# Routed experts: every token to its two experts in 39 sorted tiles, instead of all eight experts over all tokens

## The chip, the cores and the metric

One Trainium2 chip; the kernel runs on one of its cores. The metric is the device time of one execution in microseconds (us), as the median of several runs.

## What is computed

A tensor of 8 images of 16x16 tokens, 192 channels wide (2,048 tokens in all), passes through four layers: windowed attention with an MLP (layer 0), attention behind a group norm (layer 1), causal attention (layer 2) with a mixture of experts, and a last attention with a parallel block. All values are float32. The change is in the mixture of experts, which the reference computes for every token and every expert, and of which it keeps two:

```python
def _L2_ffn_ref(hidden_states, router_w, w1, w2):      # w1 (8, 512, 192), w2 (8, 192, 512)
    probs = jax.nn.softmax(flat @ router_w.T, axis=-1)
    topk_probs, topk_idx = jax.lax.top_k(probs, TOP_K)  # TOP_K = 2
    importance = probs.sum(axis=0)
    ...
    balanced = topk_probs / running[topk_idx]
    balanced = balanced / balanced.sum(axis=-1, keepdims=True)
    h = jax.nn.silu(jnp.einsum('th,eih->tei', flat, w1))
    outs = jnp.einsum('tei,ehi->teh', h, w2)
    sel = jnp.take_along_axis(outs, topk_idx[:, :, None], axis=1)
    return (sel * balanced[..., None]).sum(axis=1)
...
t = t + _L2_attn_ref(_ln_t(t), ...)
t = t + _L2_ffn_ref(_ln_t(t), ...)
t = t + _L3_attn_ref(_ln_t(t), ...)
```

## The kernel before

The kernel holds all tokens in `xall` (128 partitions x 16 rows of 192) and works on them in turns of two images, 512 tokens or 4 rows of `xall` (TURNS = 4, TT = 4). It has three parts, each a fixed order of instructions per engine, tied by semaphores.

Part A runs layers 0 to 2 up to the router. `round_a` interleaves the attention of one image (`paired`: scores, row maxima on VectorE, exponentials on ScalarE, values) with the side chains `chain_a1` to `chain_a3` of the other (projections, norms, layer 0's MLP). `chain_a3` ends with the router's probabilities in `pall`. VectorE's row maxima (`neg`) release the next scores on TensorE. GpSimd computes only 1/sqrt of the variances (`rstd_b`, `rstd_groups`) and copies for the padded windows.

The expert part is dense. After all four turns VectorE sums `pall`, TensorE sums it over partitions, and VectorE makes the weights `rrun`. Then VectorE normalises the four rows of a turn into `xd`, TensorE transposes them (`over`, L952 and L955), and for each of the 8 experts TensorE runs `up` (8 matmuls of 512 columns, four of them on half the contraction rows, weights in `moe1` and `moe1b`) and `down` (16 matmuls of 192 columns, weights in `moe2`), with `up` of the next expert ahead of `down`. A float32 matmul is two passes in the trace, so `up` is 16 and `down` 32 of them. ScalarE applies silu to four 128x512 banks per expert (L1271), VectorE multiplies with the token's weight for that expert and adds (L1908, four instructions per expert); `gates` computes these weights, zero for experts that were not chosen. All expert weights lie in SBUF: SyncE loads them once, `moe1`, `moe1b` and the first five experts of `moe2` during the last turn of part A, the other three when its last projection is done (L435 to L439). The weights of part B (`loads_b`) are loaded at the kernel's start.

Part B runs the last attention and its parallel block in the same manner as part A. `first_b` normalises the next turn's rows; its statistics on VectorE (`moments`) stand in VectorE's order ahead of row maxima. Each turn's result is stored from SyncE.

## Time and profile before

| | us |
|---|---|
| median of 3 runs | 2143.72 (2131.91 to 2151.96) |
| the profiled execution, whole | 2142.87 |
| its span in the trace | 2140.9 |
| TensorE matmul busy | 1959.9 (92%) |
| VectorE, ScalarE, GpSimd busy | 769.4, 595.4, 76.2 |
| DMA moved | 24.77 MB |

Times in the trace count from the span's start. Busy times of TensorE are of pipelined matmuls whose ends are modelled; how fast passes follow one another is read from their starts. The granted clock is the share of TensorE's full 2.4 GHz: 0.50 is 1.2 GHz. A number in brackets behind a row is the idle time of the engine before it and what ended it.

### The profile page before, as it was taken

The numbers are of one execution on the slowest core, as the hardware profiler recorded it, in microseconds if no ns is written. First come the engines' busy times: TensorE is split into PE (matmuls) and PEld (weight loads), VectorE is DVE, ScalarE is ACT, GpSimd is POOL, SyncE is SP. The second block draws the span as 40 slices with busy tenths as digits, with TensorE's granted clock in tenths as the row PEclk, the third lists the DMA queues.
The fourth block names the chain that finished last, engine by engine and source line by source line (L and its number), as shares of the span: only waits on it lengthen the run. The fifth ranks groups of instructions, "written<-read, shape, count | busy, mean of one in ns | idle before, by whom it ended". The sixth has DMA issues, their size and how long they took to land.

```text
span 2140.9 us, 35201 instructions
## 1 busy us (share of the span) xinstructions
PE 1959.9 (92%) x15802; PEld 1449.4 (68%) x15802; DVE 769.4 (36%) x1975; ACT 595.4 (28%) x919; POOL 76.2 (4%) x112
## 2 busy tenths in 40 slices
PE   6989998899989999898997899999979999999988
PEld 5767777677677776677775566666646666767666
DVE  3233334323433323432343221222125546445462
ACT  1132231332323223223222212112123434333332
POOL 0000000000000000000000000000000001000010
PEclk8799999999999999989998899999978999999999
DMA  8000000000000000000002000000010000000000
GB/s 236 1 1 1 1 1 1 1 1 1 1 1 1 1 1 1 2 1 2 1 34 86 0 1 1 1 1 0 5 35 1 1 8 1 1 8 1 9 1 8
DMA packets 8297, 24.77 MB, mean 12 GB/s; under 512 B 1001, under 2 KB 6092, under 8 KB 7155
## 3 DMA queue, kind: packets, MB, share of 16 engines
q1 hardware_dynamic: 8148, 22.54, 3.4%
q8 instruction: 124, 2.03, 0.4%
q14 instruction: 25, 0.20, 0.0%
HBM read 20.96 MB, written 1.57 MB: 11 GB/s over the span
## 4 chain that ended last, share of the span: by engine, by line
PE 83%; DVE 12%; ACT 3%; issue 1%; DMA 0%; POOL 0%; SPq 0%; DVEq 0%; ACTq 0%; POOLq 0%
PE ps L453 71%; DVE neg L1503 5%; PE ps L683 3%; PE ps L673 3%; PE ps L570 2%; ACT ring L1043 1%; PE ps L628 1%; PE ps L484 1%; PE ps L525 1%; DVE neg L1501 1%; PE ps L860 1%; PE ps L513 1%; DVE moms L1566 1%; DVE neg L1500 1%; ACT ou L1058 1%
## 5 line engine op out<-in xcount | busy, mean ns | idle before, releaser
L1043 ACT ACTIVATE ring<-ps 128x1024 f32<-128x1024 f32 (+1 forms) x240 | 232.7, 980 | 436.6 <-PE ps L453 363.6
L1503 DVE TENSOR_REDUCE neg<-ps 128x4 f32<-128x1024 f32 x192 | 234.5, 1225 | 273.3 <-PE ps L453 273.1
L453 PE MATMUL ps<-kz,qt 32*128 32x256 f32 x1152 | 167.7, 419 | 45.0 <-DVE negp L1495 22.6
L453 PE MATMUL ps<-qt,rw 128*128 128x512 f32 (+1 forms) x512 | 192.2, 632 | 0.9 <-DVE qt L1857 0.9
L453 PEld LDWEIGHTS ps<-lw,zone 128*128 128x128 f32 x1024 | 165.6, 190 | 21.2 <-issue 21.2
L453 PE MATMUL ps<-xt,lw 97*128 97x256 f32 x672 | 172.6, 409 | 7.8 <-ACT xp L1122 4.7
L453 PE MATMUL ps<-lw,zone 128*128 128x192 f32 x1024 | 174.4, 329 | 0.0
L453 PE MATMUL ps<-qm,kz 32*128 32x256 f32 x1152 | 167.6, 421 | 4.5 <-ACT pkp L1043 2.4
L453 PEld LDWEIGHTS ps<-xt,lw 97*128 97x128 f32 x672 | 130.2, 201 | 41.1 <-ACT xt L1078 9.7
L453 PEld LDWEIGHTS ps<-kz,qt 32*128 32x128 f32 x1152 | 93.9, 194 | 83.3 <-DVE neg L1503 30.2
L1908 DVE SCALAR_TENSOR_TENSOR x<-ps,cw,x 128x192 f32<-128x192 f32 x128 | 44.5, 411 | 280.1 <-PE ps L453 280.1
L453 PE MATMUL ps<-ident 128*128 128x256 f32 x472 | 144.1, 399 | 0.0
L1271 ACT ACTIVATE zone<-ps 128x512 f32<-128x512 f32 x128 | 69.5, 594 | 267.1 <-PE ps L453 267.1
L453 PEld LDWEIGHTS ps<-qt,rw 128*128 128x128 f32 (+1 forms) x512 | 64.8, 189 | 109.7 <-issue 109.7
L453 PE MATMUL ps<-rw,relt 32*128 32x256 f32 (+1 forms) x864 | 127.3, 401 | 0.7 <-ACT xt L1078 0.7
L453 PEld LDWEIGHTS ps<-qm,kz 32*128 32x128 f32 x1152 | 93.2, 195 | 23.4 <-issue 12.1
L453 PE MATMUL ps<-ring,v 128*32 128x256 f32 (+1 forms) x1536 | 103.4, 375 | 1.2 <-ACT ring L1043 1.2
L453 PE MATMUL ps<-relt,rw 32*128 32x256 f32 x768 | 103.4, 398 | 0.0
L1078 ACT ACTIVATE xt<-ps 97x512 f32<-97x512 f32 x72 | 42.9, 596 | 216.6 <-PE ps L628 216.6
L453 PEld LDWEIGHTS ps<-rw,relt 32*128 32x128 f32 (+1 forms) x864 | 86.5, 202 | 10.2 <-issue 4.0
L1305 POOL TENSOR_TENSOR rstds<-ves,nhalf 128x2 f32<-128x2 f32 x56 | 39.1, 698 | 1393.8 <-DVE ves L1573 1393.8
L453 PEld LDWEIGHTS ps<-ident 128*128 128x128 f32 x472 | 76.5, 192 | 16.4 <-issue 12.7
(228 smaller groups left out, 2809.5 us busy)
## 6 DMA issues: line engine op xcount, KB each, us to landing
lw<-in_lw SPq DMA_DIRECT2D x3, 720.0 KB
rw<-in_relw SPq DMA_DIRECT2D x1, 2048.0 KB
rw<-in_moe SPq DMA_DIRECT2D x1, 2048.0 KB, 7.6
lw<-in_moe SPq DMA_DIRECT2D x1, 1920.0 KB, 13.9
rw<-in_relw SPq DMA_DIRECT2D x1, 1792.0 KB
out<-xall SPq DMA_DIRECT2D x4, 384.0 KB, 2.6
lw<-in_lwb SPq DMA_DIRECT2D x1, 1440.0 KB
fc<-in_fc SPq DMA_DIRECT2D x2, 576.0 KB
```

Source lines behind the costliest of these rows:

```text
L453: return pe.matmul(o, w, m, start=start, stop=stop)
L484: last = pe.matmul(ps[:, b + j, half * 128:half * 256 + 128], qb[r, im, s, hs], kb[r, im, s, 0:128 + 128 * half], start=False, stop=True, ...
L513: last = pe.matmul(ps[:, b + j, half * NTOK:NTOK + half * 128], kb[r, im, s, hs], qm[r, s, half * 128:NTOK], start=False, stop=True, skip_ ...
L570: last = pe.transpose(ps[:, 5, half * 128:half * 128 + 128], neg[:, s % 2, half, :], ident[:, :])
L673: last = pe.matmul(o[:, :, k, :], rwt[:, 0, at % l.rel, :], qi[:, :, at, :], start=k == 0, stop=True, skip_group_check=True)
L683: last = pe.matmul(o[:, :, :, k], rwt[:, 1, at % l.rel, :], qi[:, :, :, at], start=k == 0, stop=True, skip_group_check=True)
L1043: act.activation(dst, src, ACT.Exp).then_inc(*q.adds("exp_done"))
L1078: act.activation(xt[:, :, im * NTOK:(im + 1) * NTOK], ps[0:CH + 1, 6:8, 0:NTOK], ACT.Copy)\
L1271: act.activation(hid2[:, 4 * (e % 2) + m, :], ps[:, m, :], ACT.Silu).then_inc(*q.adds("h_ready"))
L1305: pool.tensor_tensor(rstds2[:, part, i2], ves[:, part, i2], nhalf[:, 0:2], ALU.pow)\
L1503: ins = dve.tensor_reduce(at, ps[:, b:b + 2, :].rearrange("p j (f k) -> p j f k", f=2), AX.X, ALU.max, negate=True)
L1908: ins = dve.scalar_tensor_tensor(out=dst, in0=ps[:, 4 + 2 * (e % 2) + i // 2, (i % 2) * D:(i % 2 + 1) * D], scalar=cw[:, i, e:e + 1], in1= ...
```

## The change

The dense part goes, and a routed one takes its place. VectorE picks the two experts of each token (`choose`), TensorE counts with a triangular matrix of ones how many tokens ahead of it chose the same expert (`ranks`), and VectorE makes from it the row (`slot`) at which a token's normalised row goes in a new buffer in HBM, `rows_by_expert`: each expert has 16 tiles of 128 rows. GpSimd writes the rows there by indirect DMAs of 128 rows (`scatter`), 32 in all; the 24 of the first three turns are issued during the last turn of part A, 8 behind it. The buffer is filled with zeros first, at the kernel's start (nine stores of SyncE out of a tile that GpSimd clears). From the counts VectorE makes a `table`: for each of 39 tiles (32 full ones and up to 7 begun) its first row in the buffer and the offsets of its expert's weights. 39 tiles always run.

For each tile SyncE reads two numbers of the table into registers and fetches the tile's rows (96 KB) and its expert's first matrix (384 KB) into one of four buffers each; TensorE transposes the rows (`turn`), runs `up` (8 matmuls of 128 columns) and `down` (4 matmuls of 192 columns, whose weights it picks in `moe2` by a register); ScalarE applies silu once (128x512) and issues the store of the tile's result, back to the tile's own rows in HBM, two tiles behind (`keep`); VectorE copies out of PSUM twice per tile. When all 39 stores have landed, GpSimd gathers each token's two results by indirect DMAs, 8 per turn (`gather`), and `first_b` adds them to the token, weighted, in four instructions of VectorE per image. `loads_b` now stands between the fourth and the fifth fetch in SyncE's order.

```diff
+TILES = 2 * B * NTOK // 128 + E2 - 1
+PLACES = B * NTOK // 128
+ALL = TURNS * TT
+LATE = ALL - TT
...
+            sp.wait_ge(blank, 1)
+            for e in range(E2):
+                rows = placed_rows[e * PLACES * 128:(e + 1) * PLACES * 128, :]
+                sp.dma_start(rows.rearrange("(p n) d -> p (n d)", p=128), late[:, 0:PLACES * D]).then_inc(zeroed, 16)
...
+            sp.wait_ge(tabled, 1)
+            sp.wait_ge(scattered, 16 * 2 * ALL)
+            def fetch(k):
+                if k >= 4:
+                    sp.wait_ge(turned, k - 3)
+                place = sp.value_load(table[0:1, 0, k:k + 1], min_val=0, max_val=(PLACES * E2 + E2 - 2) * 128)
+                sp.dma_start(xin[:, k % 4, :], placed_rows[bass.ds(place, 128), :]).then_inc(tile_in[k % 4], 16)
+                if k >= 4:
+                    sp.wait_ge(up_mm, k - 3)
+                row = sp.value_load(table[0:1, 2, k:k + 1], min_val=0, max_val=CH * (E2 - 1))
+                sp.dma_start(moe1[:, k % 4, :, :], a["moe1"][bass.ds(row, CH), :, :]).then_inc(w_in[k % 4], 16)
+            for k in range(4):
+                fetch(k)
...
             for dst, src in loads_b:
                 sp.dma_start(dst, src).then_inc(ld_b, 16)
...
+            for k in range(4, TILES):
+                fetch(k)
+            sp.wait_ge(down_mm, TILES)
...
+            ranks(LATE, ALL, 2)
+            pe.wait_ge(counted, 1)
+            mm(ps[:, 6, 400:400 + E2], ones[:, :], count[:, 1, :]).then_inc(count_mm, 1)
...
+            def turn(k):
+                if k >= 2:
+                    pe.wait_ge(xts_ready, k - 1)
+                pe.wait_ge(tile_in[k % 4], 16 * (k // 4 + 1))
+                for c in range(2):
+                    last = pe.transpose(ps[0:CH, k % 2, c * 128:(c + 1) * 128], xin[:, k % 4, c * CH:(c + 1) * CH],
+                                        ident[:, :])
+                last.then_inc(turned, 1)
+            def up(k):
+                pe.wait_ge(w_in[k % 4], 16 * (k // 4 + 1))
+                if k >= 2:
+                    pe.wait_ge(hds_ready, k - 1)
+                pe.wait_ge(xts_ready, k + 1)
+                for m in range(4):
+                    for c in range(2):
+                        last = mm(ps[:, 2 + k % 2, m * 128:(m + 1) * 128],
+                                  moe1[:, k % 4, c, m * 128:(m + 1) * 128], xts[:, k % 3, c, :],
+                                  c == 0, c == 1)
+                last.then_inc(up_mm, 1)
+            def down(k):
+                first = pe.value_load(table[0:1, 1, k:k + 1], min_val=0, max_val=4 * D * (E2 - 1))
+                if k >= 2:
+                    pe.wait_ge(y_ready, k - 1)
+                pe.wait_ge(hds_ready, k + 1)
+                for m in range(4):
+                    last = mm(ps[:, 4 + k % 2, 0:D], hds[:, k % 3, m, :],
+                              moe2[:, bass.ds(first + m * D, D)], m == 0, m == 3)
+                last.then_inc(down_mm, 1)
+            pe.wait_ge(ld_moe, 32)
+            pe.wait_ge(tabled, 1)
+            turn(0)
+            turn(1)
+            up(0)
+            for k in range(TILES):
+                if k + 2 < TILES:
+                    turn(k + 2)
+                if k + 1 < TILES:
+                    up(k + 1)
+                down(k)
...
+            act.wait_ge(tabled, 1)
+            def keep(k):
+                place = act.value_load(table[0:1, 0, k:k + 1], min_val=0, max_val=(PLACES * E2 + E2 - 2) * 128)
+                act.wait_ge(y_ready, k + 1)
+                act.dma_start(placed_rows[bass.ds(place, 128), :], yst[:, k % 4, :]).then_inc(tile_out[k % 4], 16)
+            for k in range(TILES):
+                act.wait_ge(up_mm, k + 1)
+                if k >= 3:
+                    act.wait_ge(down_mm, k - 2)
+                act.activation(hds[:, k % 3, :, :].rearrange("p m t -> p (m t)"), ps[:, 2 + k % 2, :], ACT.Silu)\
+                    .then_inc(hds_ready, 1)
+                if k >= 2:
+                    keep(k - 2)
+            keep(TILES - 2)
+            keep(TILES - 1)
...
+            def scatter(t0, t1, n):
+                pool.wait_ge(placed, n)
+                for t in range(t0, t1):
+                    for k in range(2):
+                        pool.indirect_dma_start(placed_rows[:, :], bass.IndirectOffsetOnAxis(slot[:, k, t:t + 1], 0),
+                                                xl[:, t, 0:D], None).then_inc(scattered, 16)
+            def gather(turn):
+                if turn >= 2:
+                    pool.wait_ge(combined, IMGS * (turn - 1))
+                for im in range(IMGS):
+                    for i in (2 * im, 2 * im + 1):
+                        for k in range(2):
+                            pool.indirect_dma_start(
+                                gy[:, turn % 2, k, i, :], None, placed_rows[:, :],
+                                bass.IndirectOffsetOnAxis(slot[:, k, turn * TT + i:turn * TT + i + 1], 0))\
+                                    .then_inc(gathered[turn % 2][im], 16)
...
+                    if not more:
+                        scatter(im * LATE // 2, (im + 1) * LATE // 2, 1)
...
+            scatter(LATE, ALL, 2)
+            for n, landed in enumerate(tile_out):
+                pool.wait_ge(landed, 16 * len(range(n, TILES, 4)))
+            gather(0)
...
+            gather(1)
             for t in range(TURNS - 1):
                 q.stage(t, t + 1)
                 for im in range(IMGS):
                     rstd_b(q, 1, im)
                     chain_b1(q, im)
+                if t + 2 < TURNS:
+                    gather(t + 2)
...
+                if q.turn == TURNS - 1 and im == 0:
+                    choose(0, LATE)
...
+                dve.wait_ge(gathered[q.coming % 2][im], 16 * 4 * (q.coming // 2 + 1))
+                for k in range(2):
+                    for i in (2 * im, 2 * im + 1):
+                        t = q.coming * TT + i
+                        ins = dve.scalar_tensor_tensor(out=xall[:, t, :], in0=gy[:, q.coming % 2, k, i, :],
+                                                       scalar=share[:, k, t:t + 1], in1=xall[:, t, :], op0=ALU.mult,
+                                                       op1=ALU.add)
+                    ins.then_inc(*((q.adds("dve_step"), (combined, 1))[k]))
+                    dve.wait_ge(*((q.own("dve_step") if k == 0 else (combined, IMGS * q.coming + im + 1))))
...
+            after(dve.tensor_reduce(count[:, 0, :], both[:, 0:LATE, :].rearrange("p t e -> p e t"), AX.X, ALU.add))
+            choose(LATE, ALL)
+            dve.wait_ge(chosen, 2)
+            dve.tensor_reduce(count[:, 1, :], both[:, :, :].rearrange("p t e -> p e t"), AX.X, ALU.add)\
+                .then_inc(counted, 1)
...
+            read_ranks(LATE, ALL, 2)
+            place(LATE, ALL)
...
+            def turned_in(k):
+                dve.wait_ge(turned, k + 1)
+                if k >= 3:
+                    dve.wait_ge(up_mm, k - 2)
+                dve.tensor_copy(xts[:, k % 3, :, :].rearrange("p c t -> p (c t)"), ps[0:CH, k % 2, 0:256])\
+                    .then_inc(xts_ready, 1)
...
+            for k in range(TILES):
+                if k + 2 < TILES:
+                    turned_in(k + 2)
+                dve.wait_ge(down_mm, k + 1)
+                if k >= 4:
+                    dve.wait_ge(tile_out[k % 4], 16 * (k // 4))
+                dve.tensor_copy(yst[:, k % 4, :], ps[:, 4 + k % 2, 0:D]).then_inc(y_ready, 1)
```

TensorE, the expert part of before from its first transposes: `ps` is PSUM, `qt` holds the transposed tokens, `rw` and `lw` the weights, `zone` the hidden rows.

```order
L952 MATMUL ps<-ident,kz 128x128 [waits m_rows_ready,imp_done,ld_moe]
L952 MATMUL ps<-ident,kz 128x128 x3
L955 MATMUL ps<-ident,kz 128x128 x4
L453 MATMUL ps<-qt,rw 128x512 [waits m_xt1_ready,m_xt0_ready]
L453 MATMUL ps<-qt,rw 128x512 x7
L453 MATMUL ps<-qt,rw 128x512 [waits m_h_ready]
L453 MATMUL ps<-qt,rw 128x512 x3
L453 MATMUL ps<-qt,rw 128x512 [waits m_h_ready]
L453 MATMUL ps<-qt,rw 128x512 x3
L453 MATMUL ps<-lw,zone 128x192 [waits m_acc_done]
L453 MATMUL ps<-lw,zone 128x192 x15
```

TensorE now, one tile in the middle of the 39: `ring` holds the fetched and the transposed rows, the hidden rows and the results, `rw` the first matrix, `lw` all second matrices.

```order
L1029 MATMUL ps<-ident,ring 96x128 [waits tile_in1,xts_ready]
L1029 MATMUL ps<-ident,ring 96x128
L506 MATMUL ps<-ring,rw 128x128 [waits xts_ready,hds_ready,w_in0]
L506 MATMUL ps<-ring,rw 128x128 x7
L1046 TENSOR_LOAD table
L1046 ISA x2
L506 ISA [waits hds_ready,y_ready]
L506 MATMUL ps<-lw,ring 128x192
L506 ISA
L506 MATMUL ps<-lw,ring 128x192
L506 ISA
L506 MATMUL ps<-lw,ring 128x192
L506 ISA
L506 MATMUL ps<-lw,ring 128x192
```

An expert of a turn had 24 matmuls and no register work; a tile has two transposes, 12 matmuls, one load of a register and six register operations, four of them between the matmuls of `down`.

SyncE now, where the tile loop begins: the fourth fetch, `loads_b`, the fifth fetch.

```order
L480 TENSOR_LOAD table
L480 ISA x2
L481 ISA
L481 DMA ring<-rows_by_expert 128x192
L484 TENSOR_LOAD table
L484 ISA x2
L485 ISA
L485 DMA rw<-in_moe1 96x1024
L490 DMA late<-in_lwb 96x3840
L490 DMA late<-in_lwb 1x3840
L490 DMA gb3<-in_gb3 128x384
L490 DMA ties<-in_ties 128x512
L480 TENSOR_LOAD table [waits turned]
L480 ISA x2
L481 ISA
L481 DMA ring<-rows_by_expert 128x192
L484 TENSOR_LOAD table [waits up_mm]
L484 ISA x2
L485 ISA
L485 DMA rw<-in_moe1 96x1024
```

Of these rows only `loads_b` was there before, at the kernel's start; each fetch is two register loads, six register operations and two DMAs, and the transfers of `loads_b` stand ahead of the fifth fetch.

GpSimd now, from the last 1/sqrt of part A to the first turn of part B (`late` is the normalised tokens, `rw` here the buffer of gathered results).

```order
L1375 TENSOR_TENSOR rstds2<-ves,nhalf 128x2 [waits a_var_ready] x4
L1356 DMA rows_by_expert<-late,slot 17280x192 [waits placed]
L1356 DMA rows_by_expert<-late,slot 17280x192 x7
L1366 DMA rw<-rows_by_expert,slot 128x192 [waits tile_out2,tile_out3,tile_out1,tile_out0]
L1366 DMA rw<-rows_by_expert,slot 128x192 x7
L1375 TENSOR_TENSOR rstds2<-ves,nhalf 128x2 [waits b_n_var,set_b]
L1375 TENSOR_TENSOR rstds2<-ves,nhalf 128x2 [waits b_n_var]
L1366 DMA rw<-rows_by_expert,slot 128x192 x8
```

Before, one 1/sqrt per turn of the expert part (`rstd`) stood here; now 8 scatters and 8 gathers stand ahead of part B's first 1/sqrt.

## Rows read from the trace of the kernel before

**Rows 1.** Stretches: from:to, length, busy PE PEld DVE ACT POOL, clock, DMA share, GB/s
```profile
1176.00:1190.00 14.00, 6.89 (x16) 3.74 (x18) 9.18 (x42) 1.88 (x2) 1.01 (x1) 0.50 0.00 0
1200.00:1211.00 11.00, 11.00 (x50) 7.16 (x48) 1.39 (x4) 2.17 (x4) 0.00 (x0) 1.00 0.01 1
1185.60:1548.00 362.40, 362.36 (x1560) 232.29 (x1560) 74.76 (x261) 71.48 (x132) 3.02 (x3) 0.99 0.00 1
```

**Rows 2.** Timeline from the router's end to the first expert: start, us, what
```profile
1175.65 0.17 DVE L1689 TENSOR_TENSOR pall<-ge,gs 128x16 f32<-128x16 f32 x1
...
1182.80 1.09 PE L952 MATMUL ps<-ident,kz 128*128 128x128 f32 x4 [5.85 <-DVE kz L1396]
...
1183.68 1.06 PE L955 MATMUL ps<-ident,kz 128*128 128x128 f32 x4
...
1185.61 14.73 PE L453 MATMUL ps<-qt,rw 128*128 128x512 f32 x32 [0.88 <-DVE qt L1857]
```

**Rows 3.** Timeline of one expert: down, the next expert's up, the next down
```profile
1200.28 5.47 PE L453 MATMUL ps<-lw,zone 128*128 128x192 f32 x32
...
1205.58 5.91 PE L453 MATMUL ps<-qt,rw 128*128 128x512 f32 x16
...
1211.42 3.84 PE L453 MATMUL ps<-lw,zone 128*128 128x192 f32 x22
```

**Rows 4.** Timeline from the last expert to part B's first matmul
```profile
1548.08 1.39 DVE L1908 SCALAR_TENSOR_TENSOR x<-ps,cw,x 128x192 f32<-128x192 f32 x4 [3.81 <-PE ps L453]
...
1551.43 0.62 DVE L1566 BATCH_NORM_STATS2 moms<-xall 128x6 f32<-128x192 f32 x2 [0.27 <-DVE gl L1939]
...
1554.23 1.14 PE L806 MATMUL ps<-ident,xn 128*97 128x128 f32 x4 [6.26 <-DVE xn L1587]
```

**Rows 5.** Groups by shape, expert part: line, shapes, count, busy, mean ns, idle
```profile
L453 PE MATMUL ps<-lw,zone 128*128 128x192 f32 x1024 | 174.4, 329 | 0.0
```

**Rows 6.** Timeline: eight weight loads for the router's matmuls of 8 columns
```profile
1172.67 1.78 PEld L453 LDWEIGHTS ps<-rout,xt 96*128 96x128 f32 x8 [1.03 <-ACT xt L1078]
```

**Rows 7.** SyncE's stores with a register address: ns min/median/max, and landing
```profile
L445 SPq FUSED_REGOPS  x4: 74/74/84, 1747.0 to 2137.7; - x4
...
L445 SPq DMA_DIRECT2D out<-xall x4: 379/402/429, 1747.2 to 2137.8; - x4
...
DMA to landing us min/median/max: 2.6/2.6/2.7
```

**Rows 8.** Waits of SyncE: line, waited for, us in total, times, longest
```profile
SPq L274 <- DMA out<-xall: 2.1, 1, 2.1
```

**Rows 9.** Timeline: SyncE issues three loads of the expert weights, first and last
```profile
1118.15 0.33 SPq L435 DMA_DIRECT2D rw<-in_moe  x1
...
1118.99 1.31 SPq L437 DMA_DIRECT2D lw<-in_moe  x1
```

**Rows 10.** DMA issues: out<-in, engine, count, KB each, median us from issue to landing
```profile
lw<-in_moe SPq DMA_DIRECT2D x1, 1920.0 KB, 13.9
...
xall<-in_x SPq DMA_DIRECT2D x1, 384.0 KB, 3.4
```

**Rows 11.** Timeline: GpSimd in part A's last turn, two instructions in succession
```profile
995.68 1.01 POOL L1322 TENSOR_TENSOR rstd<-ve,nhalf 128x4 f32<-128x4 f32 x1 [28.52 <-DVE ve L1646]
1034.99 0.69 POOL L1305 TENSOR_TENSOR rstds<-ves,nhalf 128x2 f32<-128x2 f32 x1 [38.30 <-DVE ves L1573]
```

**Rows 12.** Timeline: the first and the last of twelve small VectorE instructions that pick experts
```profile
1186.40 0.19 DVE L1867 TENSOR_REDUCE gm<-cw 128x4 f32<-128x32 f32 x1
...
1188.86 0.19 DVE L1883 TENSOR_TENSOR oh<-oh 128x32 f32<-128x32 f32 x1
```

**Rows 13.** Timeline: part B, row maxima behind first_b of image 0 and image 1
```profile
1748.20 1.22 DVE L1503 TENSOR_REDUCE neg<-ps 128x4 f32<-128x1024 f32 x1
...
1749.47 1.13 PE L453 MATMUL ps<-lw 32*128 32x256 f32 x8 [1.03 <-DVE neg L1503]
...
1788.44 1.23 DVE L1503 TENSOR_REDUCE neg<-ps 128x4 f32<-128x1024 f32 x1 [2.27 <-PE ps L453]
```

More of the change, by code:

```diff
@@ L1646, in chain_a1 @@
                 dve.tensor_scalar(ve[0:CH, 0:2], gvar, 1e-5, None, ALU.add).then_inc(*q.adds("gvar_ready"))
+                routed = q.turn == TURNS - 1 and im == 0
+                if routed:
+                    read_ranks(0, LATE, 1)
                 yield
@@ new lines, in _ @@
+            place(LATE, ALL)
+            here, until, tile = (steps0[0:1, u:v] for u, v in ((0, PLACES), (PLACES, PLACES + E2 * E2),
+                                                              (PLACES + E2 * E2, PLACES + E2 * E2 + TILES)))
+            full = steps[:, 0:E2 * PLACES].rearrange("p (e j) -> p e j", e=E2)
+            used, ends, first, own, start, at = (spans[:, 64 * n:64 * n + z] for n, z in enumerate(
+                (E2, E2, E2 * E2, TILES, TILES, TILES)))
+            sums = first.rearrange("p (e f) -> p e f", e=E2)
```

331 lines of the change are left out of this document (147 added, 184 removed).

## Prediction

> **What bounds the kernel now.** I read the stretches first, for the size of the part that is replaced, then the timeline at its two ends and through one expert, for how its time is made up. From the first `up` at 1185.6 to the last `down` at 1548 TensorE is busy 362.36 of 362.40 us at a granted clock of 0.99, while VectorE and ScalarE stand at 75 and 71 us and nothing is transferred [rows 1]. Nobody is waited for: the 1024 passes of `down` have 0.0 us of idle time before them [rows 5]. From one `down` to the next go 11.14 us, 5.30 for its 32 passes and 5.84 for the 16 passes of the next `up` [rows 3]; 32 experts and turns make 356. So this part costs what its passes cost, and fewer passes are fewer microseconds, until something else has to be waited for. At its ends TensorE stands almost still: from `pall` at 1175.65 to the first `up` at 1185.61 [rows 2], and from the last additions at 1548.08 to part B's first matmul at 1554.23 [rows 4].
>
> **What a tile costs TensorE.** A pass of 192 columns takes 5.30/32 = 0.165 us [rows 3], so 0.86 ns a column and 0.11 for 128 columns. Could loading the weights be slower than that? The eight loads of the router's matmuls take 1.78 us, 0.22 each, with next to nothing to multiply [rows 6]; four transposes just behind, at a granted clock of 0.50 [rows 1], also take 0.22 each, from 1182.80 to 1183.68 [rows 2]. Load and 128 columns weigh the same, so 0.11 holds at full clock. A tile has 2 transposes (one pass each, 0.22), 8 matmuls of 128 columns (16 passes, 1.76) and 4 of 192 (8 passes, 1.32): 3.30 us. Between the matmuls of `down` stand four register operations of about 0.07 [rows 7], 0.3 in all, of which a part is covered by queued passes. I take 3.5 us, if nobody else is slower.
>
> **Who could be slower.** SyncE makes two fetches a tile. The trace shows the DMA with a register address at 0.40 us and a register operation at 0.074 [rows 7]; three of these and the DMA are 0.62. It does not show the load of a register from SBUF. Such a load can't be cheaper than a small instruction, 0.19 [rows 12], and, moving one word, hardly dearer than a whole DMA's wait, 2.1 [rows 8]. I take 1.0, the middle: SyncE then needs 2 x 1.62 = 3.24 us a tile, just under TensorE. At 0.19 it would be 1.6, at 2.1 it would be 5.44. TensorE's own load stands behind the 16 passes of `up` (1.76 us), which cover it if they are queued by then. ScalarE has one silu (its 71.48 us [rows 1] hold 128 of them, 0.56 each), one load and one DMA, some 2.2 us; the store waits for a copy that is two tiles old, so no silu stands behind a late one. VectorE has two copies, less than its four additions per expert before.
>
> The Trainium skill (DMA: Bandwidth & Descriptors, Latency and other measured facts) gives a register load a floor of about 600 ns. An estimate by that page makes SyncE's tile 2.4 us, TensorE stays the bound, and the sum below would lose some 1 us at the two ends. No run here shows it yet.
>
> 39 tiles of 3.5 us are 136.5. `loads_b`, 1.9 MB, now stands ahead of the fifth fetch. The three loads of expert weights (by their shapes 2,048, 1,024 and 1,920 KB, together 5.11 MB) were issued at 1118.15 to 1118.99 and the last had landed 13.9 us after its issue [rows 9, 10]: 347 GB/s, so 5.6 us for `loads_b`. The fifth tile is due four tiles, 14 us, after the first, and its fetch comes behind 2.3 MB more; I count a stall of 3 us.
>
> **The head.** From `pall` (1175.82) to the rows' places VectorE has some 20 small instructions at 0.224 from start to start [rows 12], 4.5 us, and waits in between for TensorE's count, 10 passes of 0.22 less what it covers, 1.8: 1182.1. Then 8 scatters on GpSimd. An indirect DMA is not in the trace either: below, GpSimd's smallest instruction, 0.69 [rows 11]; above, again 2.1 [rows 8]. I take 1.2, nearer the lower end, as it only writes descriptors: 9.6 us, and 2.6 until the last has landed, as the stores of 768-byte rows do [rows 7]: 1194.3. VectorE makes the table meanwhile. SyncE's first two fetches are issued by 1197.5, and 384 KB land in 3.4 us [rows 10]: first `up` at 1200.9, against 1185.61 [rows 2], 15.3 later.
>
> **The tail.** The tiles end at 1200.9 + 136.5 + 3 = 1340.4. Copy, register load and store: 2.0; landing 2.6: 1345.0. Only then GpSimd starts its gathers: four for the first image, 4.8 and 2.6 until landed: 1352.4; four additions of VectorE 1.4 (the 1.39 of four such instructions in [rows 4]): 1353.8. From there part B starts as it did, 1551.43 to 1554.23, 2.8 us [rows 4]; GpSimd's other four gathers end at 1354.6, just before its 1/sqrt is wanted. Part B's first matmul comes at 1356.6 instead of 1554.23: 197.6 us earlier.
>
> **What is added in parts A and B.** In A's last turn `ranks` costs TensorE 24 passes of 0.11, 2.6 us, uncovered, and VectorE 17 instructions of 0.224, 3.8; VectorE is idle most of that part, and I count half, 1.9. The 24 early scatters are hidden: GpSimd's next instruction comes 38.30 us after the last one [rows 11], and 12 scatters take 14.4. Without that cover each half would cost the rest. In B `first_b` gets 1.4 us of additions per image, six times behind the first turn. For image 0 they stand ahead of a row maximum for which TensorE already waits (1.03 us before 1749.47), so they count: 3 x 1.4 = 4.2. For image 1 VectorE had 2.27 us idle before its next maximum at 1788.44 [rows 13]: hidden. Later gathers have tens of us. The zero stores at the start run where nothing is transferred otherwise. Together 8.7 us.
>
> **The sum.** The profiled execution took 2142.87 us, 2 over its span and 1 under the median of 2143.72. 2142.87 - 197.6 + 8.7 = 1954.
>
> **The rivals.**
> The register load is dear: at 2.1 us SyncE needs 5.44 a tile, 39 x 1.94 = 76 and 3 at the ends: 2033. For it: nothing in the trace bounds it better. Against it: it moves one word.
> Transfers bind: a tile moves 384 + 96 + 96 KB, 590 KB. At 347 GB/s that is 1.7 us, well under 3.5. At the 141 GB/s that the 1,920 KB in 13.9 us make [rows 10] it is 4.2, 39 x 0.7 = 27 more: 1981. Against it: that load stood behind two others.
> Transfers one after the other: if each took its whole landing before the next began, 2.6 + 3.4 + 2.6 [rows 7, 10], a tile would be 8.6 us: 1954 + 39 x 5.1 = 2153, the time of before. The Trainium skill (DMA: Bandwidth & Descriptors, Rules for kernel authors) speaks for caution here: it wants at least 1 MiB per DMA and calls transfers under 64 KB mostly overhead. Against it: the three loads of [rows 9, 10] were in flight together.
> Slower: TensorE empties at each of its register loads. It then stands 2.1 us a tile, and these pauses hold its clock at 0.50, as in the sparse stretch from 1176 to 1190 [rows 1]; passes are twice as long, 6.6 + 2.1 + 0.3 = 9.0 us a tile, 1954 + 39 x 5.5 = 2168. It decides from 8.4 us a tile, where 39 x 4.9 eats the gain of 190. Against it: queued passes should cover the load, and with 3.3 of 5.4 us busy the clock need not fall.
>
> **How the numbers follow.** My forecast, a tile between 3.3 and 4.1 us, 66 in 100; dear load 18; slow transfers 11; transfers in series 2; emptied TensorE 3. Lower end: 3.3 us a tile (-8), loads at 0.19 (-2), GpSimd at 0.69 (-6), `loads_b` free (-3), parts A and B free (-9): 1926. Upper end: loads at 2.1 (+79) and GpSimd at 2.1 (+17): 2050. Faster by over 1% (what a measurement of this kernel can tell from no change) 95, within 1% 2, slower 3.
>
> **What would show it.** The profile after should have 39 silus of 128x512 some 3.5 us apart, TensorE busy over 90% in between at a clock near 1; the first `up` about 25 us behind `pall`; part B starting near 1357. If SyncE's loads bind, TensorE waits for DMA before `up` and SyncE never waits for `turned`. If transfers bind, SyncE waits and landings are long. If TensorE empties, it is idle with no releaser before each `down` and its clock falls. I would be wrong altogether if a tile took over 8 us, or if the ends took 50 us more than counted.

## The result: 2139 to 1955 us, and the profile after

The changed kernel takes 1954.9 us (median of 4, 1953.4 to 1970.6) against 2139.1 for the kernel before beside it (2131.9 to 2152.0): a ratio of 0.915, 95% interval 0.908 to 0.922. In a later round the two stood at 1964.3 and 2141.3 us, 0.917 [0.912, 0.921]; one of the changed kernel's six executions there, at 1987.3 us, fell into a slower state of the chip and is not counted. The prediction was 1954. The profiled execution took 1954.85 us, 2 over its span of 1952.8; before it was 2142.87 with a span of 2140.9.

The stretches of the changed kernel are part A in two pieces, the head (from `pall` to the first `up`), the 39 tiles, the tail (to part B's first matmul) and part B. Columns: length, then busy us and instructions of TensorE, its weight loads, VectorE, ScalarE and GpSimd, the granted clock, the DMA share, GB/s.

```profile
core 0: us, PE busy (x) PEld busy (x) DVE busy (x) ACT busy (x) POOL busy (x), PEclk, DMA share, GB/s
0.00:1100.00 1100.00, 993.52 (x9592) 781.41 (x9594) 381.61 (x934) 294.57 (x471) 64.16 (x90) 0.95 0.07 25
1100.00:1177.33 77.33, 65.79 (x582) 46.95 (x578) 26.86 (x76) 22.05 (x34) 2.09 (x3) 0.89 0.12 42
1177.33:1201.90 24.57, 4.18 (x18) 3.72 (x19) 8.51 (x38) 0.00 (x0) 7.75 (x8) 0.50 0.21 68
1201.90:1342.00 140.10, 132.39 (x1012) 130.35 (x1010) 29.20 (x87) 24.57 (x40) 0.00 (x0) 0.96 0.60 174
1342.00:1358.00 16.00, 0.08 (x1) 0.11 (x1) 3.25 (x12) 0.00 (x0) 8.36 (x9) 0.59 0.54 178
1358.00:1952.80 594.80, 541.97 (x4086) 391.35 (x4086) 290.53 (x711) 206.12 (x281) 55.18 (x63) 0.93 0.03 8
```

First `up` to last `down` is now 138.6 us (1201.93 to 1340.49) where it was 362.4 [rows 1]; TensorE is still busy in nearly all of it, but something is transferred beside it all the time, at 174 GB/s. Against that stand a head of 24.6 us from the end of `pall` (it was 9.8, [rows 2]), a tail of 17.4 (6.2, [rows 4]) and a part B of 594.9 (586.7): -223.8 + 14.8 + 11.2 + 8.2 and 1.5 in part A make the 188.1 between the spans.

The timeline of one tile in the middle of the stage, without the weight loads, which lie beside the matmuls:

```profile
1318.31 0.60 ACT L1332 ACTIVATE ring<-ps 128x512 f32<-128x512 f32 x1 [2.71 <-PE ps L506]
1318.99 0.37 ACTq L1326 DMA_DIRECT2D rows_by_expert<-ring  x1
1319.01 0.33 SPq L485 DMA_DIRECT2D rw<-in_moe  x1
...
1319.41 0.38 PE L1029 MATMUL ps<-ident,ring 128*96 128x128 f32 x2
...
1319.63 1.95 PE L506 MATMUL ps<-ring,rw 96*128 96x128 f32 x16
...
1320.11 0.33 SPq L481 DMA_DIRECT2D ring<-rows_by_expert  x1
...
1321.41 1.47 PE L506 MATMUL ps<-lw,ring 128*128 x8
1321.61 0.60 ACT L1332 ACTIVATE ring<-ps 128x512 f32<-128x512 f32 x1 [2.71 <-PE ps L506]
```

From silu to silu are 3.30 us here (3.31 over the stage), and it is TensorE's two transposes, 16 passes of `up` and 8 of `down` without a gap. ScalarE waits 2.71 us of it for TensorE. SyncE's two fetches are 1.10 us apart and then it waits for `up_mm`. What the register loads take (more than 0.15 us of register operations stands behind each), min/median/max in ns, on SyncE, ScalarE and TensorE:

```profile
L480 SPq TENSOR_LOAD <-table x39: 263/268/627, 1195.5 to 1322.7; - x39
...
L1324 ACTq TENSOR_LOAD <-table x39: 276/281/469, 1211.1 to 1340.3; - x39
...
L1046 PEldq TENSOR_LOAD <-table x39: 296/302/488, 1205.2 to 1336.9; - x39
```

The head, the stall and the tail, from the timeline. GpSimd's last scatter, SyncE's first fetch, TensorE's first transposes and first `up`:

```profile
1193.07 0.96 POOL L1356 DMA_INDIRECT rows_by_expert<-late,slot  x1 [0.30 <-issue]
1196.43 0.35 SPq L481 DMA_DIRECT2D ring<-rows_by_expert  x1
...
1198.42 0.63 PE L1029 MATMUL ps<-ident,ring 128*96 128x128 f32 x2 [14.77 <-DMA ring<-rows_by_expert]
...
1201.93 3.42 PE L506 MATMUL ps<-ring,rw 96*128 96x128 f32 x16
```

Eight scatters from 1184.14 on, 1.26 us from start to start, then SyncE's first register load starts at 1195.5, 2.4 us behind the start of the last. The granted clock is 0.50 (1.2 of 2.4 GHz) up to here, with TensorE nearly idle, and this `up` is still at half clock. The fifth tile's rows, behind `loads_b`:

```profile
1218.44 0.63 PE L1029 MATMUL ps<-ident,ring 128*96 128x128 f32 x2 [6.11 <-DMA ring<-rows_by_expert]
1218.86 3.49 PE L506 MATMUL ps<-ring,rw 96*128 96x128 f32 x16
```

TensorE stood for 6.11 us, and the 16 passes behind the pause took 3.49 us, where they take 1.95 at full clock. The tail, SyncE's `loads_ffn`, then GpSimd's first gather, its 1/sqrt behind the eighth, and part B's first matmul:

```profile
1340.53 1.13 SPq L495 DMA_DIRECT2D rw<-in_ffn  x3
...
1346.55 0.99 POOL L1366 DMA_INDIRECT rw<-rows_by_expert,slot  x1 [152.52 <-DMA rows_by_expert<-ring]
...
1356.33 0.74 POOL L1375 TENSOR_TENSOR rstds<-ves,nhalf 128x2 f32<-128x2 f32 x1
...
1357.92 1.14 PE L879 MATMUL ps<-ident,xn 128*97 128x128 f32 x4 [17.43 <-DVE xn L1662]
```

And the place in part B at which most of its 8.2 us is lost, turn 2's additions for image 0, the row maximum behind them, and TensorE's next passes, at half clock:

```profile
1552.61 1.53 DVE L1833 SCALAR_TENSOR_TENSOR xall<-rw,share,xall 128x192 f32<-128x192 f32 x4 [0.18 <-DVE xall L1947]
...
1555.19 1.22 DVE L1578 TENSOR_REDUCE neg<-ps 128x4 f32<-128x1024 f32 x1
...
1556.46 1.99 PE L506 MATMUL ps<-lw 32*128 32x256 f32 x8 [2.60 <-DVE neg L1578]
...
1562.77 3.78 PE L506 MATMUL ps<-xp,late 97*128 97x256 f32 x8
```

In [rows 13] the same 8 matmuls waited 1.03 us for the maximum and took 1.13.

### The profile page after: what moved, and what is told of

It reads as the page before. It is cut to its first block, busy times and chain, and to the rows that moved or that the text cites. A ratio compares the mean times of both kernels' runs of the same rounds, so it can differ in the third digit from the quotient of the medians.

```text
span 1952.8 us, 35144 instructions
## 1 busy us (share of the span) xinstructions
PE 1737.9 (89%) x15284; PEld 1353.9 (69%) x15284; DVE 740.0 (38%) x1856; ACT 547.3 (28%) x826; POOL 137.5 (7%) x173
## 4 chain that ended last, share of the span: by engine, by line
PE 79%; DVE 13%; ACT 3%; issue 2%; DMA 1%; POOL 1%; SPq 1%; DVEq 0%; ACTq 0%; POOLq 0%
PE ps L506 66%; DVE neg L1578 6%; PE ps L736 3%; PE ps L726 3%; PE ps L623 2%; ACT ring L1104 1%; PE ps L681 1%; PE ps L537 1%; PE ps L578 1%; DVE neg L1576 1%; PE ps L933 1%; PE ps L566 1%; DVE moms L1641 1%; DVE neg L1575 1%; ACT ou L1119 1%
## 5 line engine op out<-in xcount | busy, mean ns | idle before, releaser
L506 PE MATMUL ps<-xt,lw 97*128 97x256 f32 x480 | 129.7, 421 | 5.2 <-ACT xp L1183 3.8
L506 PEld LDWEIGHTS ps<-xt,lw 97*128 97x128 f32 x480 | 94.7, 206 | 30.7 <-issue 6.6
L506 PE MATMUL ps<-ring,rw 96*128 96x128 f32 x624 | 79.1, 282 | 0.0
L506 PEld LDWEIGHTS ps<-ring,rw 96*128 96x128 f32 x624 | 76.0, 199 | 0.0
L506 PE MATMUL ps<-lw 32*128 32x256 f32 x384 | 65.5, 466 | 11.7 <-DVE neg L1578 10.9
L1512 DVE TENSOR_TENSOR relt<-ps,relt 128x48 f32<-128x48 f32 (+4 forms) x56 | 19.4, 382 | 142.4 <-PE ps L736 142.4
L623 PE MATMUL ps<-ident,neg 128*128 128x128 f32 x240 | 50.9, 295 | 22.6 <-DVE neg L1578 15.5
L506 PEld LDWEIGHTS ps<-relt,rw 32*128 32x128 f32 x768 | 67.4, 202 | 3.3
```

Source lines behind the costliest of these rows:

```text
L506: return pe.matmul(o, w, m, start=start, stop=stop)
L623: last = pe.transpose(ps[:, 5, half * 128:half * 128 + 128], neg[:, s % 2, half, :], ident[:, :])
```

## How the runs were read

Part A is the same program in the changed kernel and in all experiments but the last two, and yet its last `pall` starts anywhere between 1177.2 us (the first trace) and 1194.1 (the second trace of the same kernel), with a granted clock of 0.95 and 0.93 up to 1100 us. Six of these traces, all of chip 5, already run from 1180.7 to 1194.1. A whole time therefore doesn't resolve an edit of 5 us, and each is read from its own stretch: over the traces of kernels that left a stretch alone, the head was 24.5 to 25.0 us from the start of `pall`, the tiles 138.6 to 139.1, the tail 17.2 to 19.0. The head was 2.0 us longer (26.8) in the two runs with more work for each fetch, sp_loads4 and weights_twice. Part B is no such stretch: from its first matmul to the end it took 590.7 to 603.2 us in nine traces that have all its additions in their place, so it is read piece by piece. Four runs price the tile stage from TensorE's, SyncE's, the DMA engines' and ScalarE's side, one moves the store to another queue; four take the stall, the tail and part B apart; two join them, and one is the changed kernel again.

## Experiments on the tile stage

### TensorE's own register load, three times

```
-                first = pe.value_load(table[0:1, 1, k:k + 1], ...)
+                for _ in range(3):
+                    first = pe.value_load(table[0:1, 1, k:k + 1], ...)
```

> TensorE loads the register for down three times a tile instead of once. Each load with its register operations takes about 0.47 us of its sequencer (0.30 and 0.15 and 0.02), 0.94 us a tile in all. Theory (passes already queued cover the sequencer): first up to last down stays at 138.6 us, 3.31 us a tile. Rival (TensorE empties at each of its register loads): 3.31 + 0.94 = 4.25 us a tile, 175 us, and more if its clock falls.

First `up` to last `down` took 151.5 us, 1969.9 in whole (2 runs). In its timeline TensorE has gaps of 0.1 to 0.2 us before `down` that nobody is named for:

```profile
1276.52 1.27 PEld L506 LDWEIGHTS ps<-lw,ring 128*128 128x128 f32 x8 [0.35 <-issue]
1276.53 1.56 PE L506 MATMUL ps<-lw,ring 128*128 x8 [0.17 <-issue]
```

Silu to silu is 3.64 us (24 of them from 1232.73 to 1320.20), so of the 0.94 us that the rows of two loads add up to 0.33 is exposed and 0.6 covered. Gaps between the register instructions, which the next run shows on SyncE, are not in the 0.94, so more may be covered than 0.6. Both expectations were off: one load is covered, as the changed kernel's gapless tile says, and three are not. So there is a limit between one and three loads. Whether it is the number of passes that can be queued, or the time that TensorE's sequencer has for a whole tile, no run separates. The clock did not fall: it was 1.00 from 1226 to 1350.

### SyncE's load, five times

```
-                row = sp.value_load(table[0:1, 2, k:k + 1], ...)
+                for _ in range(5):
+                    row = sp.value_load(table[0:1, 2, k:k + 1], ...)
```

> SyncE loads the address of a tile's weights five times instead of once. Its two fetches take 2.2 us a tile (1.10 from issue to issue), and each further load 0.44 (0.27 and 0.15 and 0.02): 3.95 us. Theory (SyncE has 1.1 us to spare in a tile of 3.31, and is the bound beyond it): 3.95 us a tile, first up to last down 138.6 + 25 = 164 us, and TensorE waits for the weights before up. Rival (the prefetch of four tiles and the queue hide it, or a register load repeated on the same word is cheaper): 139 to 145 us. If a load is as dear as the 1.0 us of the prediction, 6.2 us a tile: 250 us.

178.8 us, 2000.4 in whole. From a tile's rows to its weights SyncE now takes 3.40 us, and TensorE waits for the rows:

```profile
1271.08 0.33 SPq L481 DMA_DIRECT2D ring<-rows_by_expert  x1
...
1273.95 0.39 PE L1030 MATMUL ps<-ident,ring 128*96 128x128 f32 x2 [1.02 <-DMA ring<-rows_by_expert]
...
1274.48 0.33 SPq L486 DMA_DIRECT2D rw<-in_moe  x1
1275.58 0.33 SPq L481 DMA_DIRECT2D ring<-rows_by_expert  x1
```

3.40 - 1.10 is 2.30 for four loads: 0.575 us each from one to the next, more than the 0.44 that the three rows of a load add up to. A tile is then 1.10 + 3.40 = 4.50 us, as 1271.08 to 1275.58 shows; over the 34 tiles fetched from 1225.45 to 1379.81 it is 4.54. So the theory holds in kind (SyncE becomes the bound once it needs more than TensorE) and its size was mis-taken, because gaps between register instructions were left out. The stage grew by 40.2 us and not by 39 x 1.19, 46, since the first fetches are issued ahead of it, where the head took 2.0 us more. And TensorE waited for rows, not weights: the rows' fetch stands behind the last tile's slow weights fetch. Waits of 0.3 to 2.3 us in most tiles from 1260 to 1340 did not lower the granted clock, which was 1.00 there; from 1340 to 1360 it was 0.91.

The Trainium skill (DMA: Bandwidth & Descriptors, Latency and other measured facts) gives about 600 ns as the floor of such a load. The loads repeated on SyncE, 0.575 us from one to the next with their register operations and gaps, agree with it; the row of one load alone, 0.27, doesn't show it.

### The store from SyncE's queue instead of ScalarE's

```
+            def keep(k):      # as ScalarE's, on SyncE
...
             for k in range(4, TILES):
                 fetch(k)
+                keep(k - 4)
...
```

> The results are stored from SyncE's queue instead of ScalarE's, each behind the fetch four tiles ahead. SyncE then has three DMAs with a register load a tile; from sp_loads4 its two fetches take 2.2 us a tile, so three such steps take 3.3 us, as much as TensorE's 3.31. Theory (SyncE has just enough, and the store's wait for the copy of VectorE is met by then): 3.31 to 3.6 us a tile, 139 to 150 us. Rival (the wait for the copy stands ahead of the next fetch, and the prefetch is used up, since the copy of tile k comes 4 tiles behind the fetch that stands ahead of it): TensorE waits for rows, 4 to 4.5 us a tile, 155 to 175 us.

139.9 us for the tiles, 1969.2 in whole. SyncE's issues from the timeline:

```profile
1304.67 0.35 SPq L492 DMA_DIRECT2D rows_by_expert<-ring  x1
1305.79 0.33 SPq L481 DMA_DIRECT2D ring<-rows_by_expert  x1
1306.88 0.33 SPq L485 DMA_DIRECT2D rw<-in_moe  x1
1307.97 0.36 SPq L492 DMA_DIRECT2D rows_by_expert<-ring  x1
```

Three steps of 1.10 us are 3.30, exactly a tile, with nothing to spare: most silus are 3.31 us apart, but four of the later ones are 3.4 to 4.0 apart. As the theory had it, ScalarE's queue is not what makes the tile cheap; it is what leaves SyncE a third of its time.

### The store directly behind its own silu

```
-                if k >= 2:
-                    keep(k - 2)
+                keep(k)
```

> ScalarE stores a tile's result directly behind its own silu instead of two tiles later, so it waits for that tile's down and copy before the next silu. From the trace: down of a tile ends 3.97 us after its silu ends (1318.91 to 1322.88), the copy 0.4 later, the DMA 0.37, the next silu 0.60: it ends about 5.5 us after the last, at 1324.4, and the next down wants it at 1324.6. Theory (the time of a tile is TensorE's passes as long as that chain is under 3.31 us plus what up covers): 3.31 to 3.6 us a tile, 138.6 to 150 us. Rival (the distance of two tiles is what keeps ScalarE's queue from binding): 5.5 us a tile, 220 us.

144.7 us, 1976.3 in whole. Each silu now waits for VectorE's copy instead of for TensorE:

```profile
1244.08 0.60 ACT L1332 ACTIVATE ring<-ps 128x512 f32<-128x512 f32 x1 [2.83 <-DVE ring L2049]
```

A tile is 3.40 us, in the range expected. The chain through copy and store, which was expected to fit with 0.2 us to spare, is 0.1 us too long; the lag of two tiles in the changed kernel is worth 39 x 0.1, with the pauses at the ends 6 us, and not 80.

### The weights fetched twice

```
-                sp.dma_start(moe1[:, k % 4, :, :], a["moe1"][bass.ds(row, CH), :, :]).then_inc(w_in[k % 4], 16)
+                for dst in (moe1, spare):
+                    sp.dma_start(dst[:, k % 4, :, :], a["moe1"][bass.ds(row, CH), :, :]).then_inc(w_in[k % 4], 16)
...
```

> Each tile's 384 KB of weights are fetched a second time, into columns of rw that nothing uses in this stage; TensorE waits for both. A tile then moves 983 KB; at 3.31 us this is 297 GB/s, against 174 at a DMA share of 0.60 now, and 347 GB/s in the load before the stage. Theory (transfers have room beside TensorE's passes): 138.6 to 143 us, at most 3.4 us a tile, DMA share near 1. Rival (transfers are near their bound as it is, so 174 GB/s is what they give): 983 KB at 174 are 5.65 us a tile, 220 us.

151.2 us, 1983.4 in whole. Here are 42 us in the middle of the stage, for which the changed kernel has a DMA share of 0.61 and 175 GB/s, and then the landings from 1230 to 1350:

```profile
1262.00:1304.00 42.00, 41.36 (x312) 38.42 (x311) 9.24 (x24) 7.17 (x12) 0.00 (x0) 1.00 1.06 282
```

```profile
rw<-in_moe SPq DMA_DIRECT2D x64, 384.0 KB, 8.8
rows_by_expert<-ring ACTq DMA_DIRECT2D x33, 96.0 KB, 8.0
ring<-rows_by_expert SPq DMA_DIRECT2D x31, 96.0 KB, 9.5
```

The DMA engines are full (share 1.06) and a transfer lands after 8 to 9.5 us instead of 3 to 4. By the silus a tile takes 3.31 us until 1261, 3.52 from there to 1303 (12 tiles) and 3.7 to 4.4 in the twelve after, 3.9 on average. So here the transfers are the bound, and the theory's 3.4 was too low. The stall behind `loads_b` grew too, by 3 us, so that the stage missed the expected 143 us by 8. But it is a bound at 1.6 times the changed kernel's rate, 282 against 175 GB/s, and until it is reached the four tiles fetched ahead cover landings of 9 us. This also disposes of the prediction's case in which short transfers go one after another.

## Experiments on the stall, the tail and part B

### `loads_b` behind the last fetch

```
-            for dst, src in loads_b:
-                sp.dma_start(dst, src).then_inc(ld_b, 16)
             for k in range(4, TILES):
                 fetch(k)
+            for dst, src in loads_b:
+                sp.dma_start(dst, src).then_inc(ld_b, 16)
```

> loads_b is issued behind the last fetch instead of between the fourth and the fifth. Theory (the 6.11 us in which TensorE stood at 1218.44, and the half clock of the 16 passes behind it, 3.49 us instead of 1.95, both come from the fifth fetch queued behind 1.9 MB): the idle time before the fifth tile's transposes falls from 6.11 us to under 1, no passes at half clock after the first two tiles, first up to last down 138.6 - 7.6 = 131 us, whole 1947 us. Rival (the first four tiles were fetched too late anyway and loads_b only fills a hole: the tiles are fetched at 2.2 us each, their landing takes 2.9 to 3.6): the idle time stays over 3 us, 136 us, whole 1952. Part B's start is as before, since loads_b lands 6 us before it is wanted; if it collides with the last fetches, the tail grows by up to 3 us.

130.8 us from first `up` to last `down`: 7.8 less, as the theory had it. The silus are 3.31 us apart from the third on, and no transposes wait. The tail was 0.5 us longer, within what it wanders. The whole time, 1959.6 against 1947 expected, shows nothing of the gain: in this trace part A was 4.7 us longer and part B 8.3 us, at places that the edit doesn't touch.

### `loads_ffn` behind the gathers, and the 1/sqrt between them

```
+            sp.wait_ge(gathered[0][IMGS - 1], 16 * 4)
             for dst, src in loads_ffn:
...
-            gather(0)
+            gather(0, [0])
             for im in range(IMGS):
+                if im:
+                    gather(0, [im])
                 rstd_b(q, 1, im)
```

> SyncE waits for the gathered rows of turn 0 before it issues loads_ffn (2 MB), and GpSimd gathers image 0's rows, makes its 1/sqrt, and then gathers image 1's. Theory (the last stores landed only 5.1 us after the last issue because loads_ffn, issued at the same moment, takes the DMA engines; GpSimd's 1/sqrt stood behind four gathers that nobody waited for yet): last store to first gather 2.7 us instead of 5.1, the 1/sqrt 0.7 us earlier; from the last down to part B's first matmul 17.4 - 3.1 = 14.3 us. But image 1's four gathers then stand in front of nothing that is late: part B goes on as it did. Rival (the stores' landing is long by itself: the median landing in the middle of the stage is 3.7 us): 16.7 us. Whole 1952 or 1954.

13.8 us instead of 17.4, 1951.4 in whole. The last `down` ended at 1357.21 in this trace, the gathers began at 1360.31, and `loads_ffn` was not in their way:

```profile
1360.31 0.99 POOL L1367 DMA_INDIRECT rw<-rows_by_expert,slot  x1 [150.08 <-DMA rows_by_expert<-ring]
...
1369.47 0.73 POOL L1376 TENSOR_TENSOR rstds<-ves,nhalf 128x2 f32<-128x2 f32 x1 [4.40 <-DVE ves L1651]
...
1371.05 1.14 PE L880 MATMUL ps<-ident,xn 128*97 128x128 f32 x4 [13.84 <-DVE xn L1665]
```

From the last `down` to the first gather went 3.1 us instead of 6.1, and the 1/sqrt started 0.25 us behind the start of the instruction that makes its input, instead of 0.83. Image 1's gathers started 10 us later than image 0's, and part B lost nothing by it.

### The additions moved, and left out

```
             def first_b(q, im):
-                (wait for gathered, four additions)
+                if q.coming < 2:
+                    combine(q, q.coming, im)
...
             def chain_b2(q, im):
...
+                if q.turn + 2 < TURNS:
+                    combine(q, q.turn + 2, im)
                 dve.wait_ge(*q.next("ffn2_mm"))
```

> The additions of turns 2 and 3 (four of 128x192 an image) are made one turn earlier, ahead of VectorE's wait for ffn2_mm, where it stands idle for 6.95 us; turns 0 and 1 are as they were. Theory (image 0's additions stand ahead of the row maximum for which TensorE waits: 1.57 us each, and the longer pause drops TensorE's clock to half for the next 24 passes): turn 2's image 0 gives back the 5.9 us that were lost near 1555 to 1570, turn 3's 1.5 us; part B 594.9 - 7.4 = 587.5 us, whole 1947.5. Rival (part B is longer because its clock differs from trace to trace, or because something else moved): part B stays at 592 to 595 us.

> The additions of turns 1 to 3 are left out altogether (turn 0's stay), so the output lacks the experts' part of these turns; the gathers, their waits and all the rest stay. It prices what moved_adds moves, and turn 1's with it. Theory: part B 586.7 us as in the kernel before (594.9 - 8.2), of which turn 1 gives 1.5; whole 1946.5. If moved_adds gives back as much as this but turn 1's 1.5 us, its new place costs nothing. Rival (additions are not the cause): 592 to 595 us here too.

Part B took 583.7 us with the additions moved and 589.4 with them left out; in whole 1957.3 and 1955.4, which can't tell them apart. Expected were 587.5 and 586.7. The pieces can. From the 1/sqrt before turn 2's image 0 to its own (1474.00 to 1555.36 in the changed kernel's trace) go 81.36 us with the additions in their place, in 17 of 18 such pieces of nine traces (one has 81.95), and 79.87 with them moved, in 6 of 6: 1.5 us each, for turns 2 and 3. The kernel before has 79.79. Left out, they gave back less, 80.26 and 80.50; why is open. In their new place they cost VectorE 1.37 us of the 6.95 for which it waited there:

```profile
1528.63 1.52 DVE L1832 SCALAR_TENSOR_TENSOR xall<-rw,share,xall 128x192 f32<-128x192 f32 x4
1535.74 0.75 DVE L1948 TENSOR_TENSOR zone<-ps,gate 128x48 f32<-128x48 f32 x4 [5.58 <-PE ps L506]
...
1566.64 1.13 PE L506 MATMUL ps<-lw 32*128 32x256 f32 x8 [1.10 <-DVE neg L1578]
```

The larger part is the next piece, from this 1/sqrt to the next one. It takes 10.15 us or 14.5, and the longer one is the one with TensorE's passes at half clock: its granted clock is 0.65 over the piece, that of the shorter one 1.00. With the additions ahead of the maximum it was the longer one 17 times of 18, and once it was 11.21, at a clock of 0.85; without them ahead it was the longer one 3 times of 10, once each in the kernel before, in no_adds and in all_four below. So the clock fell behind every wait of 2.6 us, but also behind some of 1.0 to 1.5. The wait goes with the fall, worth 4.35 us, far more often, and is not the only thing that decides it. What decides it in the others is open. For image 1 the additions add 1.57 us in one piece (24.31 instead of 22.74) and take 1.56 from the next (11.11 instead of 12.67): hidden, as predicted.

## The changed kernel again, and two that join the gains

> The changed kernel once more, beside all_four on the same chip. Nothing differs from before, so every difference between its two traces is what one execution differs from another by: expected 0.1 us between the stretches in which nothing but the stage's own work counts (head 24.8, tiles 138.6, tail 17.4 us), but up to 15 us in part A and 8 in part B, as between the traces of late_loads_b, tail and moved_adds, whose part A is the same program.

Its trace had 24.5, 139.0 and 17.7 us for head, tiles and tail, up to 0.4 us from the first where 0.1 was expected, `pall` 17 us later and part B 5.4 us longer. The five executions counted went from 1954 to 1978 us, median 1964.3.

The next kernel joins the three edits above and changes the head twice: the last turn's image 0 is ranked and scattered on its own, and the first fetches are ordered anew.

```
+MID = ALL - 2
...
+            for k in range(4):
+                weights(k)
             sp.wait_ge(scattered, 16 * 2 * ALL)
+            for k in range(4):
+                rows(k)
...
-            scatter(LATE, ALL, 2)
+            scatter(LATE, MID, 2)
+            scatter(MID, ALL, 3)
```

> late_loads_b, tail and moved_adds together, and the head shortened: the first four tiles' weights are fetched while the last scatters run, and the last turn's image 0, whose probabilities are there 22 us before image 1's, is ranked and scattered ahead of image 1's, so that four scatters instead of eight stand behind the last probabilities. Theory, each part from its own stretch: head 24.8 - 4 x 1.26 - 1.1 = 18.7 us, tiles 138.6 - 7.8 = 130.8, tail 17.4 - 3.6 = 13.8, part B 594.9 less 3.1 (the additions' own time) to 11.2 (with the half clock behind them) = 584 to 592. In all 20.6 to 28.7 us under the changed kernel: 1926 to 1934 us. Rival (the gains are taken back elsewhere, as the earlier weights collide with the scatters' own transfers, or the extra ranking stands in TensorE's way before the last probabilities): 1940 us or more, and a head of 22 us or more.

1938.6 us (6 runs, 1929 to 1953), 0.905 [0.901, 0.909] of the kernel before, and 26 us under the changed kernel on the same chip, where 20.6 to 28.7 were expected; the 1926 to 1934 us in whole were missed. Tiles 130.9, tail 13.8, part B 586.4, as expected; the head 20.6 instead of 18.7. Its first fetches and TensorE's first transposes:

```profile
1198.15 3.65 SPq L483 DMA_DIRECT2D rw<-in_moe  x4
1202.59 6.24 SPq L479 DMA_DIRECT2D ring<-rows_by_expert  x5
1207.11 1.06 PE L1036 MATMUL ps<-ident,ring 128*96 128x128 f32 x4 [13.82 <-DMA ring<-rows_by_expert]
```

The table that names the weights is ready only as the last scatter starts, so nothing was gained by the new order, and the rows came behind 1.5 MB. The last kernel takes that order back:

> all_four with the order of the first fetches as in the changed kernel again: a tile's rows, then its weights, all behind the last scatter. In all_four the first rows were fetched at 1202.59 us, behind four weight fetches issued from 1198.15 on, and TensorE's first transposes came at 1207.11, 4.5 us later; in the changed kernel's trace the same step took 2.0 us. Theory (the first rows were late because 1.5 MB of weights were in transfer ahead of them, and the earlier ranking gave its 6.3 us, from 16.9 to 10.6 us between the last probabilities and the last scatter's end): head 24.8 - 6.3 = 18.5 us instead of 20.6, the rest as in all_four (130.9, 13.8, and 584 to 592 for part B); 2 us under all_four. Rival (the rows are late for another reason, such as the scatters' own landing): head 20.6 us again.

```profile
1201.30 0.35 SPq L482 DMA_DIRECT2D ring<-rows_by_expert  x1
...
1203.34 0.63 PE L1033 MATMUL ps<-ident,ring 128*96 128x128 f32 x2 [9.57 <-DMA ring<-rows_by_expert]
```

The head is 18.6 us, the step from the first fetch to the transposes 2.0 instead of 4.5. Span 1934.1; 1939.3 us in whole (6 runs, 1922 to 1948), 0.905 [0.901, 0.910], which no run can tell from all_four. Both are faster than the changed kernel's 0.917 [0.912, 0.921] and, though these intervals just touch, its 0.915 [0.908, 0.922]. The stretches say by 6.2 (head), 7.9 (stall) and 3.6 us (tail). Part B was 8.5 and 12.2 us under the first trace, of which the pieces show 3 us for the additions in their new place and 4.35 for each piece at full clock instead of half.

## Why the prediction was right, step by step

The time came out within 1 us, and the mechanism is the one forecast: fewer passes, and everyone else covered. That it hit so closely is luck, since its terms were off by up to 8 us in both directions.

- **TensorE's tile.** The passes were predicted at 3.30 us and measured at 3.31. The 0.2 us for register operations was wrong: they are wholly covered, 39 x 0.19 = 7.4 us too much. Three loads instead of one show the cover's end.
- **SyncE and the register load.** Predicted 1.0 us a load and 3.24 us a tile, close to TensorE's. Measured 0.27 for the instruction, 0.575 from load to load, 1.10 a fetch and 2.2 us a tile. The order of who bounds was right, with more room than thought. The case of a dear load (18 in 100) would have needed a fetch 2.5 times as long; the experiment with five loads is what it looks like.
- **Transfers.** Predicted room, found: at 1.6 times the present rate a tile takes 3.5 to 3.9 us instead of 3.31.
- **`loads_b`.** The 3 us were the most mis-sized term: 6.1 us of waiting and some 1.5 for the passes at half clock behind it, 7.8 when taken away. The landing was predicted well: 3 us behind the 14 is 17 us behind the first `up`, and TensorE had the rows after 16.5. What was wrong is the 14. A tile's transposes stand two tiles ahead of its `up` in TensorE's order, so the fifth tile's rows were wanted behind the second `down`, at 1212.33, only 10.4 us after the first `up`. The clock behind the wait was left out as well. The error cancels against the tile's 7.4.
- **The head.** Predicted 25.1 us from `pall`'s end, measured 24.6. A scatter was put at 1.2 us, and is 0.96 busy and 1.26 from start to start; its landing was counted 2.6 from its end and was done about 1.5 behind it. From the first weights' fetch to the first `up` went 4.4 us instead of 3.4: the weights landed after 3.7, and the second tile's transposes, which stand ahead of `up` in TensorE's order, got their rows only at 1201.47.
- **The tail.** Predicted 16.2, measured 17.4. The landing of the last stores was taken at 2.6 us in an idle chip, but `loads_ffn` starts at the same moment; and the 1/sqrt, put just in time, came 0.6 us late behind the gathers. The range's 17 us for an indirect DMA of 2.1 us were also too many: eight scatters and four gathers at 0.9 more are 11, and about 14 with the 1/sqrt behind all eight gathers.
- **Part A.** Predicted 4.5 us, measured 1.5 between the two traces, against a wander of 17: neither is shown.
- **Part B.** Predicted 4.2 for three additions, measured 8.2 between two traces, which alone shows little in a part that wanders by 12. The pieces show more. The place was right, and about the size, 1.7, 1.6 and 1.6 us for the three, but the clock behind the longer wait was not in the sum: 4.3 us in turn 2. Pieces that vary between traces gave 1.0 back. Image 1's were hidden, as predicted.
- **The slower rival.** Emptied TensorE needed a pause at each load and a clock of 0.50. The clock in the stage, once past the stall, is 1.00, also with three loads, and SyncE's five loads, which did make TensorE wait in most tiles, left it at 1.00 for 80 us. What the register loads could not do, a single wait of 6.1 us did for 16 passes.

## What to carry to other kernels

When a stage is moved from computing everything to fetching what is needed, count each queue's steps a tile from start to start, gaps and all, and compare them with the passes: here 3.3 us of passes stood over 2.2 of SyncE, and the design was safe by a third. The losses then sit at the ends and at bulk loads that share a queue or the DMA engines with something urgent; move those behind the last urgent one. Ask too when a prefetched buffer is first wanted in the engine's own order, not when its tile is computed. And a short wait put ahead of TensorE should be priced with the half-clock passes that may follow: here 1.6 us of added wait went with 4.35 us of them.

## What was new about the hardware

- An indirect DMA of 128 rows of 768 bytes keeps GpSimd for 0.96 us and comes every 1.26 us; the last of eight scatters had landed 2.4 us after its start.
- A register load of a word from SBUF takes 0.27 to 0.30 us as an instruction, and 0.575 from one to the next on SyncE; a fetch with one load costs the queue 1.10 us.
- One register load a tile on TensorE costs nothing beside its passes, three do: of 0.94 us of further register work 0.33 was exposed.
- The same program's part A differs by 17 us between two executions; what the traces show to differ is the granted clock (0.95 and 0.93 up to 1100 us).
- A piece of part B takes 10.15 us at a granted clock of 1.00 and 14.5 at 0.65: 14.5 in 17 of 18 cases behind a wait of TensorE of 2.6 us, in 3 of 10 behind one of 1.0 to 1.5 us.
- Waits of TensorE of 0.3 to 2.3 us in most tiles of 4.5 us left the clock at 1.00 for 80 us (five loads on SyncE, 1260 to 1340).
